# Raw copy and strip cast of the convolution moved from VectorE to ScalarE in a macaron block with a gated delta rule

## The reference

```python
def attn(x):                        # x: layer norm of the residual
    q, k, v = x @ Wq.T, x @ Wk.T, x @ Wv.T
    q, k, v = causal_dwconv(q), causal_dwconv(k), causal_dwconv(v)   # 4 taps per channel
    g = log_sigmoid(x @ Wg.T); beta = sigmoid(x @ Wb.T)
    k = k / norm(k); q = q * Kd ** -0.5
    for t in range(T):              # per head, S is 64 x 64
        delta = outer(v[t] - S @ k[t], k[t])
        S = exp(g[t]) * S + beta[t] * delta
        o[t] = S @ q[t]
    return o @ Wo.T

x = x + 0.5 * ffn(layernorm(x))
x = x + attn(layernorm(x))
x = x + 0.5 * ffn(layernorm(x))
```

## Time and profile before

| | us |
|---|---|
| median of 2 timed runs | 3956.37 |
| lowest and highest | 3951.47, 3961.27 |
| the profiled execution | 3964.82 |
| its span on the slowest core (core 2) | 3963.3 |
| spans of the 8 cores | 3929.4 to 3963.3 |
| PE busy | 1242.1 |
| DVE busy | 1300.8 |
| ACT busy | 397.5 |

### The profile page before, as it was taken

One profiled execution on the slowest core, in us unless ns is written; L12 is line 12 of the kernel. 1 busy time (PEld: TensorE's weight loads), 2 busy tenths in 40 slices (PEclk: granted clock), 3 DMA queues, 4 the chain that ended last, 5 costly groups with the idle time before them and its releaser, 6 DMA issues.

```text
span 3963.3 us, 34990 instructions; the slowest of 8 cores (3929.4 to 3963.3 us)
## 1 busy us (share of the span) xinstructions
PE 1242.1 (31%) x12064; PEld 619.7 (16%) x12112; DVE 1300.8 (33%) x2463; ACT 397.5 (10%) x1033; POOL 232.8 (6%) x314
## 2 busy tenths in 40 slices
PE   0554313321143333112342331033333210332254
PEld 0111001111121111112120111031201110221011
DVE  1222214344521244454122344531134444321221
ACT  0225100011000001110000011000000110000021
POOL 2000000000100000001000000000000001000100
PEclk9775555555555555555555555555555555555677
DMA  5001112201712221018213210262222105112102
GB/s 129 3 0 40 47 24 29 30 7 11 20 22 43 43 32 22 9 9 20 38 27 53 27 18 9 23 10 38 38 43 27 15 9 25 22 27 38 43 0 85
DMA packets 288894, 114.31 MB, mean 29 GB/s; under 512 B 207376, under 2 KB 264864, under 8 KB 288704
## 3 DMA queue, kind: packets, MB, share of 16 engines
q0 software_dynamic: 139504, 70.91, 17.9%
q1 hardware_dynamic: 112224, 32.70, 3.5%
q10 hardware_dynamic: 36992, 8.46, 1.1%
HBM read 146.87 MB, written 26.08 MB: 44 GB/s over the span
## 4 chain that ended last, share of the span: by engine, by line
PE 30%; DVE 24%; DMA 23%; issue 12%; ACT 5%; ACTq 2%; DVEq 1%; POOL 1%; SPq 1%; POOLq 0%
PE pp L250 30%; DMA wring<-woT 8%; DMA wring<-wqT 2%; DMA wring<-wkT 2%; DMA wring<-wvT 2%; DVE subtmp L943 2%; DMA scr_tc<-tcst 1%; ACTq L273 1%; DMA lgT<-scr_flat 1%; DMA wb<-scr_w 1%; ACT cacc L658 1%; DVE cacc L950 1%; DVE cacc L661 1%; DVE cacc L667 1%; DVE cacc L664 1%
## 5 line engine op out<-in xcount | busy, mean ns | idle before, releaser
L250 PE MATMUL pp<-x2s,wring 128*128 128x512 bf16 x752 | 335.4, 622 | 582.3 <-DMA wring<-wqT 110.2
L250 PE MATMUL pp<-wring,oT 128*128 128x512 bf16 x240 | 113.3, 623 | 386.4 <-DMA wring<-woT 386.4
L250 PEld LDWEIGHTS pp<-x2s,wring 128*128 128x128 bf16 x768 | 99.6, 139 | 817.6 <-issue 817.6
L649 DVE COPY rawt<-pp 128x512 f32<-128x512 f32 x96 | 66.4, 691 | 401.9 <-PE pp L250 401.9
L658 ACT ACTIVATE cacc<-rawt,cconvb,cconvw 128x512 f32<-128x512 f32 x96 | 78.0, 813 | 1044.0 <-DVE rawt L649 1044.0
L250 PE MATMUL pp<-big,xTt 128*128 128x512 bf16 x496 | 169.9, 501 | 26.1 <-ACT xTt L457 24.2
L1220 DVE TENSOR_TENSOR R<-R,pp 128x512 f32<-128x512 f32 x32 | 20.6, 684 | 468.4 <-PE pp L250 468.4
L250 PE MATMUL pp<-ci,xln 128*128 128x128 bf16 x384 | 79.4, 257 | 302.3 <-ACT xTt L457 250.1
L250 PE MATMUL pp<-stripB,stripA 16*16 16x16 bf16 x2048 | 53.9, 167 | 356.1 <-DMA stripB<-scr_t16t 306.4
L1169 ACT ACTIVATE Sb<-Sm 128x512 bf16<-128x512 f32 x32 | 20.1, 629 | 1320.5 <-DVE Sm L1166 1320.5
L481 DVE SCALAR_TENSOR_TENSOR R<-pp,R 128x512 f32<-128x512 f32 x64 | 44.3, 692 | 300.8 <-PE pp L250 300.8
(11 more groups left out here) (153 smaller groups left out, 2374.9 us busy)
## 6 DMA issues: line engine op xcount, KB each, us to landing
wring<-woT POOLq DMA_DIRECT2D x64, 512.0 KB, 5.1
x2s<-scr_x2t SPq DMA_DIRECT2D x8, 1024.0 KB, 7.3
wring<-wqT POOLq DMA_DIRECT2D x16, 512.0 KB, 5.7
wring<-wkT POOLq DMA_DIRECT2D x16, 512.0 KB, 5.6
wring<-wvT POOLq DMA_DIRECT2D x16, 512.0 KB, 5.6
out<-R SPq DMA_DIRECT2D x16, 512.0 KB, 6.6
R<-x ACTq DMA_DIRECT2D x8, 512.0 KB, 12.2
R<-x POOLq DMA_DIRECT2D x8, 512.0 KB, 10.5
```

The lines of the kernel that those rows point to most:

```text
L250: return e.matmul(out, lhsT, rhs, start=start, stop=stop, tile_position=tp)
L649: e_raw = self.dve(lambda e, pb=pb: e.tensor_copy(self.rawt[:, 3:3 + 512], pb[:, 0:512]), deps=(ev_last,))
```

## The change

Two instructions of each group move from DVE to ACT: the raw copy out of PSUM (L649) and the cast into the strip (L670, L671 after the change). Both become an activation with the function Copy. What they read and write is the same, and what waits for them is the same.

```diff
-                e_raw = self.dve(lambda e, pb=pb: e.tensor_copy(
-                    self.rawt[:, 3:3 + 512], pb[:, 0:512]), deps=(ev_last,))
+                e_raw = self.act(lambda e, pb=pb: e.activation(
+                    self.rawt[:, 3:3 + 512], pb[:, 0:512], AF.Copy),
+                    deps=(ev_last,))
...
-                ev_sp = self.dve(lambda e, w=w, ct=ct, strips=strips: e.tensor_copy(
-                    strips[w][:, ct * 512:(ct + 1) * 512], self.cacc[:]), deps=(e_c3,))
+                ev_sp = self.act(lambda e, w=w, ct=ct, strips=strips: e.activation(
+                    strips[w][:, ct * 512:(ct + 1) * 512], self.cacc[:], AF.Copy),
+                    deps=(e_c3,))
```

## The result

| | us |
|---|---|
| before, median (31 runs beside the changed kernel) | 3958.2 |
| after, median (32 runs) | 3966.1 |
| ratio, 95% interval | 1.0021 (1.0012 to 1.0029) |
| forecast ratio (3971.3 over 3956.4) | 1.0038 |

The changed kernel is slower by 0.2%, some 8 us (5 to 12). That is no change by the 2% of the forecast, and it has the forecast's sign, but only a bit over half of its 14.9 us.

A forecast was written before the change was run, and what follows sets the result against it. The prediction took the q, k, v matmuls to be bound by waits for weight DMAs and the convolution chain. It added 4.3 + 10.6 = 14.9 us to the median 3956.4, giving 3971.3 us, range 3960 to 3983, widened to 3951 to 3991.

The forecast's parts named there:

- The bound: In the q, k, v projections, matmuls wait about 47 times for a weight DMA, 48 times for the convolution's end.
- the 48: Groups whose matmuls wait for the convolution, 5.1 us each; each tenth of a microsecond on its chain is paid 48 times.
- the cover of the other half: In groups waiting for a weight DMA, the convolution has 1.30 us to spare, so a longer chain costs 0.
- Part 1: Raw copy to ACT in the convolution's chain: shorter copy and handoffs, -.12 us a group.
- Part 2: Cast to ACT at the chain's end: cast .20 longer, PE's start .01 later, +.21 us a group.
- Part 3: At four slab ends, three DMA issues queue behind the moved cast; L720 starts 2.64 us late, 10.6 us in all.
- The sum: Whole kernel: 4.3 us from the longer chain plus 10.6 us at slab ends, 14.9 us slower.
- The held issues count: Rival at slab ends said they do not: DMA issues go out as before, +2.5 us, 3958.9 us; chance .05.
- The cast did not leave the path: Rival said it would: next matmuls go once the third multiply-add is done, 31 us less, 3936; chance .02.
- No table was loaded for Copy: Rival said alternating Copy and Identity on ACT load two function tables per group, +208 us, 4164; chance .01.
- Slower handoffs: Rival: each of the chain's three seams .1 us dearer, 14.4 us more, 3985.7 us; chance .07.
- The activation pair that closes up: Rival: no .09 us gap between raw copy and e_c0 on ACT, 4.7 us less, 3966.6 us; chance .09.

The follow-up runs named there:

- e7: Kernel before, with each weight DMA released by the last matmul that used its buffer, two pairs ahead: ratio 0.9830 to the kernel before.
- e2: Kernel before with only the raw copy moved to ACT, the cast staying on DVE: ratio 0.9992 to the kernel before.
- e5: Kernel before with the first matmul of a group taking its waits in turned order, ACT's first and DVE's last: ratio 0.9994 to the kernel before.
- e6: Changed kernel with the first matmul's waits in turned order, ACT's first and DVE's last: ratio 1.0043 to the kernel before.
- e3: Kernel before with only the cast moved to ACT, the raw copy staying on DVE: ratio 1.0033 to the kernel before.
- e1: Changed kernel with the three DMA issues of a slab's first chunk recorded behind e_c0, ahead of the last cast: ratio 0.9986 to the kernel before.
- e4: Kernel before with the first DMA issue of a slab's first chunk also waiting for the cast on DVE: ratio 1.0027 to the kernel before.
- p2: Kernel before with early weights, free DMA issues, matmuls not waiting for the convolution, one buffer, raw copy and cast on ACT: 3540.8 us, ratio 0.8929.
- p5: Kernel before with early weights, free DMA issues, matmuls not waiting for the convolution, two buffers, raw copy and cast on DVE: 3447.9 us, ratio 0.8695.
- p4: Kernel before with early weights, free DMA issues, matmuls not waiting for the convolution, two buffers, raw copy and cast on ACT: 3383.6 us, ratio 0.8542.
- p1: Kernel before with early weights, free DMA issues, matmuls not waiting for the convolution, one buffer, raw copy and cast on DVE: 3539.4 us, ratio 0.8925.

## Why the prediction was right or wrong

**The bound: right.** Half of the groups wait for weights, half for the chain, and the 48 decide. e7 showed the cover of the other half: with it gone they wait for the chain as the 48 do, 5.05 us.

**Part 1, the raw copy: right.** -.12 was told, -.10 measured in a plain group of e2. The copy takes .60 against .69, and the seam behind the matmuls is .09 instead of .11. The seam to `e_c0` stayed at .10. What the part left out is the first group of each slab, which gained .2 more, under 1 us in all.

**Part 2, the cast: this is the step that failed.** The cast is .20 longer, as told. What failed is "PE started .25 after the DVE cast and .26 after the ACT cast", with +.01 drawn from it. The earlier trace rows are of another place. The first matmul there has further waits in its list behind the one for ACT, so by what e5 and e6 showed it also pays for them; that last step is read from the code and was not tried. Behind the moved cast the seam fell from .25 to .14, so part 2 cost .09 (e3) instead of .21, and parts 1 and 2 together came to -.02 instead of +.09. Over the 48 groups that is -1.0 instead of +4.3 us, and with the first groups of the slabs and the stray ones -2.3. The size of one seam was wrong, and with it the sign of the term. That the forecast still has the right sign is due to part 3, the larger term.

**Part 3, the held DMA issues: right, in mechanism and size.** Told: L720 2.64 us late in each slab, 10.6 in all. Measured from the start of the last multiply-add to the last step of the lgT split, median of the cores: 2.42, 2.70, 2.70 and 2.75 us more in the four slabs, 10.6; the multiply-add itself is .1 earlier, so 10.2 remain. e1 took it away, e4 put it into the kernel before.

**The sum.** 10.2 - 2.3 = 7.9 us, against 8.3 (4.8 to 11.5) measured (0.0021 x 3958). The rows account for the time within the interval. They could not do so more closely, since the 44 weight waits alone scatter by some 3 us between kernels.

**The rivals.** The held issues count (e1, e4). The cast did not leave the path. No table was loaded for Copy. Slower handoffs: the opposite. The activation pair that closes up did not come: `e_c0` starts .10 behind the end of the raw copy (598.50 to 598.60). The Trainium skill ("ScalarE: Activation LUTs", section "What ACT_TABLE_LOAD costs") states that back-to-back activations overlap by about 93 ns. The traces agree where the second does not wait for the first: in p2 the raw copy starts at 614.40, .10 before the cast ahead of it ends at 614.50. Where it does wait, they show the gap of .10.

## What to carry to other kernels

Before work is moved between engines, ask whether anybody waits for the engine or only for the step. In a chain that goes through all engines one after another the move is worth the difference of the row lengths and seams; the same move gave 1.9% once the chain was cut and DVE alone was the bound. Then look at the queue that receives the work: what stands behind a moved instruction that waits, DMA issues above all, waits with it. And in PE's list of waits, put the one that ends last at the end.

## What the runs showed of the hardware

**A met wait behind the last one costs .11 us on PE** (e5, e6). I had taken seams to belong to pairs of engines.

**TensorE was granted a higher clock where its gaps were shorter.** The granted clock in the q, k, v step of slab 0, first of the kernel before (columns: window, its length, busy us of PE, PEld, DVE, ACT, POOL with counts, granted clock, DMA share, GB/s):

```profile
570.00:800.00 230.00, 81.17 (x184) 24.44 (x189) 88.91 (x163) 18.69 (x23) 10.57 (x12) 0.57 0.23 33
```

and of p5 on its core 5, in the middle of that step:

```profile
585.00:645.00 60.00, 33.41 (x141) 12.48 (x138) 54.81 (x115) 13.63 (x17) 7.00 (x8) 0.99 0.58 72
```

Before, PE was busy 35% of the stretch, in bursts of 3.6 us with 5 to 7 us between them, at .57 of full speed, so for most of the time at the lower of its two levels (1.2 and 2.4 GHz). In p5 it was busy 56% of the stretch, 8 matmuls in every 3.6 us, and was granted .99, the upper level for nearly all of it; in p4 it was granted .82 to .91 on the 8 cores in the same 60 us. What of the new order brought the clock up, no run separates. The time of a matmul follows, in p4 (least, median, most ns):

```profile
L254 PE MATMUL pp<-x2s,wring x768: 376/379/634, 571.6 to 2523.7; 128*128 128x512 bf16 x192
```

Its median was 634 ns before; with one buffer it was 396 in p1 and 380 in p2. None of this was in my expectation of p4, where PE was to be the bound at 3.6 us a group. At the upper level 8 matmuls take 1.89 us, as this row of p5 shows, and that is how DVE could be the bound at 2.77:

```profile
614.60 1.89 PE L254 MATMUL pp<-x2s,wring 128*128 128x512 bf16 x8 [1.76 <-DVE tails L679]
```

The clock was not part of the change itself: it was .56 to .57 on all cores before and after.
